# Rest rows of two batches scored as one tile, and the next queries written one step sooner

## The reference

```python
q = _split_heads(query @ Wq.T + bq, B, Q)
k = _split_heads(key @ Wk.T + bk, B, KV)
v = _split_heads(value @ Wv.T + bv, B, KV)
scores = jnp.einsum('bhqd,bhkd->bhqk', q, k) / SCALE
top_scores, top_idx = jax.lax.top_k(scores, eff_k)
w = jax.nn.softmax(top_scores, axis=-1)
top_v = jnp.take_along_axis(v[:, :, None, :, :], top_idx[..., None], axis=3)
out = jnp.einsum('bhqk,bhqkd->bhqd', w, top_v)
```

## Time and profile before

| | |
|---|---|
| median of 3 runs | 2232.36 us (2230.2 to 2232.58) |
| the profiled execution | 2234.97 us, its span 2233.1 us |
| TensorE matmul busy | 2013.7 us, 90% |
| VectorE busy | 1887.9 us, 85% |
| ScalarE busy | 1322.6 us, 59% |
| GpSimd busy | 1297.5 us, 58% |
| mean granted TensorE clock | 0.957 |

### The profile page before, as it was taken

The page is one execution under the profiler, slowest core; times in us unless marked ns, Lnnn a source line. Parts: engine busy times, 40 slices in busy tenths (PEclk is TensorE's granted clock), DMA queues, the critical chain, the costliest instruction groups (busy, mean ns, idle before and its releaser), DMA issues.

```text
span 2233.1 us, 50537 instructions
## 1 busy us (share of the span) xinstructions
PE 2013.7 (90%) x19824; PEld 1565.1 (70%) x19824; DVE 1887.9 (85%) x3502; ACT 1322.6 (59%) x2640; POOL 1297.5 (58%) x1566
## 2 busy tenths in 40 slices
PE   4899999999987889899899999999989989999966
PEld 2566666666664778787787777877878778777753
DVE  6567575757544799999999999999999999999994
ACT  4333333333322577777777777777777767777753
POOL 6465656556533365666656656666566665665642
PEclk8899999999988999999999999999999999999977
DMA  6000000000046100010001000010000000100000
GB/s 197 13 16 20 16 20 16 20 17 20 16 141 143 31 19 14 26 31 22 19 21 39 19 22 26 14 39 19 21 28 30 21 19 21 39 19 21 8 2 12
DMA packets 41959, 70.40 MB, mean 32 GB/s; under 512 B 4689, under 2 KB 21345, under 8 KB 41722
## 3 DMA queue, kind: packets, MB, share of 16 engines
q1 hardware_dynamic: 37226, 59.73, 8.6%
q0 software_dynamic: 2736, 4.16, 1.0%
q10 hardware_dynamic: 1760, 3.28, 0.5%
HBM read 60.54 MB, written 9.86 MB: 32 GB/s over the span
## 4 chain that ended last, share of the span: by engine, by line
PE 46%; ACT 11%; issue 6%; DVE 3%; POOL 2%; DMA 1%; ACTq 0%; POOLq 0%; another core or an unknown queue 0%; DVEq 0%
PE ca_pF L88 7%; PE ca_pF L89 6%; PE ca_pF L90 6%; PE ca_pT L1229 4%; PE ca_pO L1276 4%; PE ca_pS L88 3%; PE ca_pS L90 3%; PE ca_pS L89 3%; PE ca_pX L1331 3%; PE ca_pX L1295 2%; PE ca_pX L1322 2%; ACT ca_W L1383 2%; ACT ca_top L1386 2%; ACT ca_S L1400 2%; ACT ca_S L1393 1%
## 5 line engine op out<-in xcount | busy, mean ns | idle before, releaser
L1603 DVE MATCH_REPLACE8 ca_W<-ca_top,ca_W 128x722 f32<-128x722 f32 (+1 forms) x624 | 553.9, 895 | 0.0
L1592 DVE MAX8 ca_top<-ca_W 128x8 f32<-128x722 f32 (+1 forms) x624 | 537.4, 899 | 1.7
L1074 POOL TENSOR_TENSOR ca_S<-ca_S,ca_W 128x722 f32<-128x722 f32 (+1 forms) x208 | 358.7, 1744 | 120.8 <-ACT ca_W L1383 120.8
L1052 POOL TENSOR_TENSOR ca_KL<-ca_K,ca_KH 128x384 fp32r<-128x384 f32 (+1 forms) x128 | 122.8, 959 | 196.4 <-ACT ca_KH L1375 193.8
L88 PE MATMUL ca_pS<-ca_KH,ca_QH 128*128 128x362 f32 (+1 forms) x384 | 148.7, 387 | 90.4 <-ACT ca_S L1400 85.8
L1393 ACT ACTIVATE ca_S<-ca_S,ca_shift 128x722 f32<-128x722 f32 (+1 forms) x208 | 175.8, 891 | 65.3 <-POOL ca_shift L1066 65.2
L1583 DVE MAX8 ca_top<-ca_S 128x8 f32<-128x722 f32 (+1 forms) x208 | 181.0, 901 | 36.0 <-ACT ca_S L1400 35.6
L1405 ACT ACTIVATE ca_PT<-ca_pT 128x768 f32<-128x768 f32 (+1 forms) x208 | 163.0, 784 | 67.2 <-PE ca_pT L1229 62.9
L341 POOL TENSOR_TENSOR sa_ss<-sa_ss,sa_minus_half 100x16 f32<-100x16 f32 x64 | 190.0, 2984 | 20.9 <-DVE sa_ss L528 20.9
L1383 ACT ACTIVATE ca_W<-ca_W,ca_shift 128x722 f32<-128x722 f32 (+1 forms) x208 | 186.7, 897 | 10.0 <-DVE ca_W L1603 10.0
L1400 ACT ACTIVATE ca_S<-ca_pS 128x722 f32<-128x722 f32 (+1 forms) x208 | 159.7, 768 | 55.0 <-PE ca_pS L90 54.5
(11 more groups left out here) (225 smaller groups left out, 5203.3 us busy)
## 6 DMA issues: line engine op xcount, KB each, us to landing
ca_raw<-in_ctxT SPq DMA_DIRECT2D x32, 384.0 KB, 4.2
ca_raw<-in_ctxT SPq DMA_DIRECT2D x32, 338.0 KB, 3.2
sa_xin<-in_x SPq DMA_DIRECT2D x16, 200.0 KB
sa_xres<-in_x SPq DMA_DIRECT2D x16, 200.0 KB
x_scratch<-sa_x SPq DMA_DIRECT2D x16, 200.0 KB
x_scratch<-y_scratch POOLq DMA_DIRECT2D x16, 200.0 KB, 13.9
ca_xin<-x_scratch SPq DMA_DIRECT2D x16, 200.0 KB
ca_x<-x_scratch SPq DMA_DIRECT2D x16, 200.0 KB
```

The lines of the kernel that those rows point to most:

```text
L1074: pool.tensor_tensor(S[k][rows, :], S[k][rows, :], W[r][rows, :], ALU.subtract).then_inc(p_ready, 1)
L1592: n_of[t.i] = order.mark(dve.max(top[r][rows, 8 * k:8 * k + 8], W[r][rows, :]))
L1603: ins = dve.match_replace(W[r][rows, :], eight, W[r][rows, :], REMOVED)
```

## The change

Rest tiles now exist only in even batches. The one of batch b (even) holds 128 rows: for each g the 16 rest rows of batch b and the 16 of batch b + 1 (`PAIR` = 128). An odd batch has six steps with tiles; its step 6 still does what prepares the next batch. `RUN` lists the steps that have tiles, and the rings of buffers go by places in it.

The rest queries are kept whole, in plain 32 bits, in two buffers RQ, one a parity, where the other batch's columns are zero (ScalarE, `rest_query`, in step 2). `rest_score` adds four terms into each strip of 32 output partitions: high and low part of the keys of batch b with its RQ, and the same of batch b + 1. Contraction is over partitions 96 to 127 alone; strip g gets set g. So the pair needs all keys of batch b + 1 at the end of step 5 of batch b. In those batches slice 7 is projected at the first place of step 4 (`PAIR_PLAN`). The rest scores are made late in step 5, behind slice 10. In step 5 of an odd batch the next batch's two first tiles are scored late in the step. For this the queries are split in step 4, not 5. The rest output of the second batch waits in `second_rest`, and ScalarE puts it in place in step 2 after next.

```diff
+    PAIR_PLAN = [([12], [13]), ([], [0, 1]), ([2], [3]), ([4, 5], [6]), ([7], [8, 9]), ([10], []), ([], [11])]
...
+        RQ = [sb(f"RQ{p}", [128, 4, 2 * REST]) for p in range(2)]
...
 # GpSimd, body
                     for x in cur:
                         shifts(*x)
-                    if s == 5 and tiles and nxt:
-                        query_low(bn)
                     for x in first + second:
...
+                    if s == 4 and tiles and nxt:
+                        query_low(bn)
                     if s == 4 and prev:
                         pool.wait_ge(xn2_ready, b.count(1, 0))
                         pool.tensor_tensor(x2[:, :], x2[:, :], bias_f[:, :], ALU.add).then_inc(x2f_ready, 1)
...
 # TensorE
+            def rest_score(tb, tp, t):
+
+                nb = tb.next()
+                pe.wait_ge(rq_ready, nb.count(1, 1))
+                pe.wait_ge(k_lo, nb.count(8, 8))
+                pe.wait_ge(s_ready, position(tb, t.i))
+                terms = [(p, k) for p in (tp, 1 - tp) for k in (KH, KL)]
+                for keys, cols in KEYS:
+                    for n, (p, k) in enumerate(terms):
+                        for g in range(4):
+                            last = pe.matmul(pS[DH * g:DH * g + DH, cols], RQ[p][3 * DH:128, g, :],
+                                             k[p][3 * DH:128, g, keys].bitcast(F32), start=n == 0, stop=n == len(terms) - 1)
+                last.then_inc(s_mm, 1)
...
+                    swap = s == 5 and tiles
+                    if coming and not swap:
                         score(*coming[0])
...
                     if len(old) > 1:
                         weights_T(*old[1])
+                    if swap and not b.const % 2:
+                        rest_score(*coming[0])
+                        if prev:
+                            spectral()
+                    if swap and b.const % 2 and coming:
+                        score(*coming[0])
+                        values(*old)
                     if len(coming) > 1:
                         score(*coming[1])
...
 # ScalarE, body
+                    if swap and coming:
+                        keep_scores(*coming[0])
                     if len(coming) > 1:
                         keep_scores(*coming[1])
+                    if s == 4 and tiles and nxt:
+                        high_query(bn, position(b, NT - 1))
+                    if s == 2 and prev and not b.const % 2:
+                        act.wait_ge(ot_ready, b.count(GROUPS, -1))
+                        act.wait_ge(second_ready, b.const // 2)
+                        act.activation(ctxT[3 * DH:128, :, T - REST:T], chunks(second_rest, 4), ACT.Copy).then_inc(ot_ready, 1)
...
 # VectorE, body
-                        if k == 3 and s == 1 and prev:
+                        if k == 3 and s == 1 and prev and b.const % 2:
```

More of the change, by code:

```diff
@@ L785, in __init__ @@
         self.g, self.t = divmod(i, 3)
-        self.rows = 4 * self.REST if self.rest else 128
         self.dims = 128 if self.rest else 2 * DH
@@ new lines, in score @@
+                if t.i == 0:
+                    pe.wait_ge(q_lo, tb.count(4, 4))
+                if t.t == 0:
+                    pe.wait_ge(k_lo, tb.count(8, 5 + t.g))
+                need(pe, s_ready, position(tb, t.i))
+                rows = slice(128 * t.t, 128 * t.t + 128)
+                for keys, cols in KEYS:
+                    last = split3(pe, pS[:, cols], QH[:, t.g, rows], QL[:, t.g, rows],
+                                  KH[tp][:, t.g, keys], KL[tp][:, t.g, keys], True, True)
@@ L1231, in weights_T @@
                 last.then_inc(pt_mm, 1)
             def rest_values(tb, tp, t):
[L1235 to L1245 removed]
+                r = slot(tb, t)
@@ new lines, in rest_values @@
+                pe.wait_ge(pt_ready, done(tb, t.i))
+                pe.wait_ge(rz_ready, done(tb, t.i))
+                pe.wait_ge(o_kept, kept(tb, GROUPS - 1))
+                pe.wait_ge(kv_out, tb.next().count(NSL, NSL))
+                pe.matmul(pO[3 * DH:128, DEN:DEN + PAIR], rZ[:, r:r + 1].broadcast_to((128, DH)), ident[:, :],
+                          start=True, stop=True)
+                for p in (tp, 1 - tp):
+                    for g in range(4):
+                        at = 2 * REST * g + REST * p
+                        for k in range(KC):
+                            last = pe.matmul(pO[3 * DH:128, NUM + at:NUM + at + REST],
+                                             V[p][:, k, 128 * g + 3 * DH:128 * g + 128],
+                                             PT[0][:, k, at:at + REST], start=k == 0, stop=k == KC - 1)
@@ L1448, in body @@
                         exps_left(*x)
-                    if s == (5 if tiles else 2) and nxt:
-                        need(act, s_mm, b.count(NT, NT - 1 if tiles else 0))
-                        act.wait_ge(q_ready, bn.count(CC, CC))
-                        for h in range(4):
-                            rows = slice(DH * h, DH * h + DH)
-                            act.activation(QH[rows, :, T * h:T * h + T], qT[rows, :, :], ACT.Copy).then_inc(q_hi, 1)
-                    if coming:
+                    if s == 2 and not tiles and nxt:
+                        high_query(bn, 0)
+                    swap = s == 5 and tiles
+                    if coming and not swap:
                         keep_scores(*coming[0])
@@ L1590, in body @@
                                 else:
                                     order.after(n_of[t.i])
-                                n_of[t.i] = order.mark(dve.max(top[r][rows, 8 * k:8 * k + 8], W[r][rows, :]))
+                                n_of[t.i] = order.mark(dve.max(top[r][:, 8 * k:8 * k + 8], W[r][:, :]))
                         for tb, tp, t in cur:
-                            r, rows = ring(t, tp), slice(0, t.rows)
-                            eight = top[r][rows, 8 * k:8 * k + 8]
+                            r = ring(tb, t)
```

297 lines of the change are left out of this document (139 added, 158 removed).

## The result

The changed kernel takes 2359.6 us (median of 4 runs, 2356.4 to 2363.2) against 2232.0 for the kernel before, run beside it: the ratio is 1.056, 95% interval 1.053 to 1.059. That is 128 us slower, where 27 were forecast, and above the range. The profiled execution has a span of 2361.4 us against 2233.1.

The account below looks back on a forecast made before the run. VectorE's picking plus what happens around rest steps was taken to bound the cross-attention part. Removed 68.1 us, added 82 at even batches' ends and 12.6 at odd ones: +26.5, forecast median 2259 us, range 2212 to 2286.

Parts of the forecast that it names:

- the odd rest steps and the removed product: Between batches: seven odd rest steps go, 60.1 us less; fewer small products after step 1, 1 us less.
- the end of an even batch: VectorE begins the pair 9.6 us late, plus 0.8 behind it: 82 us added in all, ends 34 and 120.
- the odd boundary: From an odd batch into the next: 1.8 us of waits seven times, 12.6 us added, ends 9 to 28.
- The prediction's own worst ends: Upper ends of two added terms: 120 us at even batches' ends, 28 us at the odd boundary.
- The pair's scores: TensorE's 32 matmuls in step 5 of even batches: 4.9 us in eight rounds plus 1.8 for the clock, 6.7 us.
- The key slice: GpSimd's last low key slice in even batches would end 15.6 us after VectorE's step 5 begins.
- The tail: Last batch, without its rest tile: some 10.5 us from the picks to the y matmuls instead of 17.5, 7 less.
- half clock throughout the scores and more lag: Rival at the pair's scores: 3 to 4 us more eight times, 2287 us; no separate chance given.
- Late but little: Rival: TensorE and ScalarE enter even batches' step 4 early, key slice little late; 2207 to 2222 us, chance 0.22.
- No overlap: Rival: the pair's four score strips run serially, 19.4 instead of 4.9 us; 2375 us, chance 0.04.

Follow-up runs that it names:

- the first experiment: The changed kernel with the pair's scores taking only the even batch's own keys, so without the wait for the next batch's keys: 2245.4 us, ratio 1.005.
- the filled wait: The changed kernel with the six transposes ahead of the pair's scores made 16 times over in even batches: 2333.8 us, ratio 1.046.
- The combined kernel: The changed kernel with only the last two score rounds waiting, the second rest part copied early, and GpSimd reordered in steps 4 and 5: 2209.1 us, ratio 0.990.
- the early copy: The changed kernel with ScalarE copying the second rest part before step 2's score copies in even batches: 2352.9 us, ratio 1.0538.

## Why the prediction was wrong

The sign and the mechanism were right: the even batches pay for a pair that waits on the next batch's last key slice, behind GpSimd's queries, bias product and weights; the 61 us for the odd rest steps and the removed product are in the trace as worked out. What failed is the size of what the change adds: the end of an even batch, put at 82 us, takes 160 (122, 22 and 16), and the odd boundary, put at 13, takes 38. The prediction's own worst ends, 120 and 28 us, come to 2312, yet its range stopped at 2286; the measured time lies above both. The terms:

- **The pair's scores, 6.7 us put, 9.8 measured** (1021.09 to 1030.87). I took 4.9 for the rounds, which the first experiment shows (5.0 in batch 2), and 1.8 for the clock, calling 4.9 the end of the range. The trace has the whole of it at 0.50: behind the idle stretch the clock didn't come back in all eight rounds, and the filled wait shows it falling in them even when it is up at their start. This gives 3 us of the 5.6 that are missing from each wait. Behind the pair the spectral product took 5.7 us and not 3.6, which with its last matmul I had put at 4.0; that term is 22 us, not 6. The combined kernel shows what the clock has in it: where the product ran at full clock there, the first wait behind the pair was 1.7 us shorter. In the changed kernel no batch has that, and its waits follow the product's time (3.47 us behind 5.44, 4.38 behind 6.35).
- **The key slice, 15.6 us into step 5 put, 17.9 measured**, the other 2.3. I had ScalarE begin the query copies 3.75 us before step 5 and GpSimd end the third key slice 3.0 us into it. The copies begin 1.7 us before:

```profile
1001.42 2.20 ACT L1460 ACTIVATE ca_QH<-ca_qT 32x400 fp32r<-32x400 f32 x4
```

  The exps and key copies behind them are as much later, and GpSimd, after 4.10 us of waiting for them, ends the slices 5.8 us into the step. ScalarE trails here because the second tile's score of step 4 does: the 15 us of waits in step 4, which I had at nothing. Over half of these go with the early copy, which the prediction counted only at the far end of its range. That this lag makes the slice late is argued from the order of the rows; with it gone in one batch of the early copy the pair still waited 14.6 us, so it is at most a small part of the 2.3, and the rest stays open.
- **The odd boundary, 1.8 us put, 5.4 measured.** The bias product ended 22.8 us after step 4 began, put at 22.0. Then the clock counted again: TensorE idled 2.31 us for it, and the last spectral matmul and the projection ran at 0.60:

```profile
1117.37 3.60 PE L1319 MATMUL ca_pX<-ca_M,ca_xT 128*100 128x512 f32 x8
1123.27 1.59 PE L1321 MATMUL ca_pX<-ca_x,ca_ident 100*100 100x512 f32 x2 [2.31 <-POOL ca_x L1162]
```
```profile
1123.30:1127.60 4.30, 4.30 (x14) 0.60 0.01 4
```

  From the start of that last matmul to the end of the projection are 4.39 us, put at 2.8: 1.6 us, twice the 0.8 by which the bias product was late. The second tile waits 2.06 and not 1.5. Both ends of my range (9 to 28) lay under the 38 measured.
- **The tail, 10.5 us put, 13.7 measured.** The last step's picks end at 2325.0 and the y matmuls begin at 2338.66. TensorE stands 6.41 us there, because the copy of the transposed weights of the tile before waits in ScalarE's order behind the last picks' exps; up to the y matmuls it then works at half clock (PEclk 0.50 from 2327.2 to 2338):

```profile
2327.27 0.39 PE L1293 MATMUL ca_pO<-ca_ident,ca_rZ 128*32 128x44 f32 x6 [6.41 <-issue]
```

Of the rivals, *half clock throughout the scores and more lag* had the right mechanism, but priced it at 3 to 4 us a time, 2287, since it took the clock in the pair's scores alone and left the odd boundary as it was. *Late but little* needed TensorE and ScalarE to lead VectorE in step 4 of even batches; the waits there show that they trail it. *No overlap* is out: rounds of 0.61 us. The 2.38x for three column tiles that the Trainium skill states ("TensorE: Matmul & The Clock Gate", section "Measured speedup vs the span model") doesn't hold for this kernel's four strips: one 362-column matmul alone is, by estimate from the earlier trace rows, 0.86 x 362/512 = 0.61 us, and four side by side take 0.61, four times the rate.

What stays open: why the clock held behind the pair in batches 6 and 10 of the combined kernel and fell in the others, what made the key slice late by most of its 2.3 us, and how much of the early copy's 5 to 7 us is more than the noise.

## What to carry to other kernels

When work that needs a late operand is merged with work that doesn't, wait for that operand only ahead of the part that reads it: here two rounds of eight, 50 us alone, and 75 together with the early copy once the order was good. Price a wait of TensorE by what runs behind it at half clock, and not by its own length. And before an engine's items are moved, see which of its waits the moved item could fill: on the kernel before, the queries' move to step 4 cost 23 us with GpSimd's four products behind the key slices; ahead of all but the first slice they ran in what had been a wait of 4.1 us.

## What the hardware showed that I had not expected

TensorE's clock fell with the engine busy. In the first experiment, batch 4, there is no idle time right ahead of the pair's eight rounds of 32-row, 32-column strips (the last pause, of 1.59 us, ends 13 us before them), and they begin at 0.61 us each; from the fifth on they take 1.20:

```profile
1191.92 0.84 PE L1240 MATMUL ca_pS<-ca_KL,ca_RQ 32*32 32x362 f32 x8
1192.53 1.43 PE L1240 MATMUL ca_pS<-ca_KH,ca_RQ 32*32 32x360 f32 x8
```
```profile
1190.00:1192.50 2.50, 2.50 (x34) 1.00 0.07 20
1192.50:1197.50 5.00, 5.00 (x37) 0.50 0.00 0
```

In batch 2 of that run, and in most batches of the combined kernel, all eight rounds ran at full clock and the spectral product right behind them took 5.4 us instead of 3.60. In batches 6 and 10 of the combined kernel it took 3.68: the fall isn't certain. In the filled wait, 1.33 us of idle time behind 10.67 us of transposes, the seventh round of batch 2 took 1.20. The Trainium skill, in "TensorE: Matmul & The Clock Gate", section "Why this matters for your kernels", names gaps between bursts of matmuls as what takes the clock down. The changed kernel's 11.07 us gap agrees with that; the first experiment and the combined kernel show a fall with no gap right ahead, and there the measurement decides. That the strips' shape is the cause is not shown, since no run puts wider matmuls in their place. In the changed kernel the clock was back at 1035 us, 4 us after the strips' end, within the spectral product.
